# First attention: the split of the finished maxima on GpSimd instead of VectorE, and the turn of their rows four halves later

## The reference

```
B, S, D = hidden_states.shape            # 2, 1024, 128;  H = 16 heads of hd = 8
qkv = hidden_states @ w_attn + b_attn
q, k, v = split, reshaped to (B, H, S, hd)
scores = einsum('bhqd,bhkd->bhqk', q, k) * hd ** -0.5
scores = scores + mask        # -log(1 + k - q) for keys after the query, 0 at it, -inf before it
attn = softmax(scores, axis=-1)
out = (attn @ v) reshaped to (B, S, D) @ w_proj + b_proj
```

## Time and profile before

| | us |
|---|---|
| median of 3 runs | 1112.68 |
| lowest, highest | 1106.85, 1120.25 |
| the profiled execution's own time | 1102.42 |
| its span, first to last instruction | 1100.3 |
| busy in the span: PE, PEld | 896.0, 606.8 |
| busy in the span: DVE, ACT, POOL | 665.8, 427.8, 512.2 |
| mean granted TensorE clock | 0.887 of full |

### The profile page before, as it was taken

The page is one execution under the profiler, slowest core; times in us unless marked ns, Lnnn a source line. Parts: engine busy times, 40 slices in busy tenths (PEclk is TensorE's granted clock), DMA queues, the critical chain, the costliest instruction groups (busy, mean ns, idle before and its releaser), DMA issues. The chain is left out here.

```text
span 1100.3 us, 17965 instructions
## 1 busy us (share of the span) xinstructions
PE 896.0 (81%) x6334; PEld 606.8 (55%) x6334; DVE 665.8 (61%) x1876; ACT 427.8 (39%) x1024; POOL 512.2 (47%) x463
## 2 busy tenths in 40 slices
PE   4668999999999867267899699994998987389992
PEld 2122333333333356155566588994895756389982
DVE  6767778686872075879687656778003666533334
ACT  2323665565666441113111276774334211032220
POOL 5425888888898831053222344555200001156661
PEclk9657999899999988758799799997999998599997
DMA  4800110110000000001000000302000001266764
GB/s 146 257 1 1 31 31 2 30 30 19 13 2 24 1 22 8 0 15 40 1 2 1 10 21 10 134 9 77 1 1 1 1 10 30 89 188 216 217 196 145
DMA packets 38893, 55.95 MB, mean 51 GB/s; under 512 B 6954, under 2 KB 26290, under 8 KB 38678
## 3 DMA queue, kind: packets, MB, share of 16 engines
q1 hardware_dynamic: 36310, 49.70, 14.9%
q0 software_dynamic: 2496, 5.12, 1.6%
HBM read 43.66 MB, written 10.94 MB: 50 GB/s over the span
## 5 line engine op out<-in xcount | busy, mean ns | idle before, releaser
L423 POOL TENSOR_TENSOR arena<-arena 128x1024 f32<-128x1024 f32 (+3 forms) x105 | 201.0, 1946 | 42.4 <-ACT arena L598 42.3
L665 DVE CUSTOM_DVE_ANT_0 ps<-ps,arena 128x512 f32<-128x512 f32 (+3 forms) x256 | 148.7, 640 | 45.3 <-PE ps L480 44.4
L598 ACT ACTIVATE arena<-ps 128x512 f32<-128x512 f32 (+3 forms) x320 | 137.3, 491 | 89.4 <-PE ps L511 58.1
L480 PE MATMUL ps<-arena 48*128 48x512 bf16 (+3 forms) x384 | 103.9, 371 | 24.9 <-DVE arena L665 15.9
L117 POOL TENSOR_SCALAR vareps<-meanvar 128x4 f32<-128x4 f32 x32 | 7.9, 246 | 213.2 <-DVE meanvar L98 213.2
L503 PE MATMUL ps<-arena 51*128 51x512 bf16 (+3 forms) x384 | 76.0, 349 | 6.0 <-DMA arena<-arena 5.2
L2075 PE MATMUL ps<-arena 128*128 128x128 f32 x624 | 79.9, 284 | 0.0
L480 PEld LDWEIGHTS ps<-arena 48*128 48x128 bf16 x384 | 28.3, 95 | 91.3 <-DVE arena L665 55.1
L2075 PEld LDWEIGHTS ps<-arena 128*128 128x128 f32 x624 | 76.4, 200 | 0.0
L152 PE MATMUL ps<-ident,xn 128*128 128x128 f32 x128 | 26.0, 352 | 59.4 <-DVE x L921 19.9
L532 PE MATMUL ps<-arena 128*9 128x512 f32 (+3 forms) x640 | 67.7, 495 | 3.9 <-POOL arena L423 3.9
(11 more groups left out here) (341 smaller groups left out, 2081.0 us busy)
## 6 DMA issues: line engine op xcount, KB each, us to landing
arena<-in_L_ffn_w SPq DMA_DIRECT2D x39, 512.0 KB, 3.7
arena<-scratch SPq DMA_DIRECT2D x32, 192.0 KB, 4.0
arena<-in_L_ffn_w SPq DMA_DIRECT2D x16, 256.0 KB, 3.4
scratch<-arena SPq DMA_DIRECT2D x12, 256.0 KB, 4.4
arena<-expert_rows SPq DMA_DIRECT2D x8, 256.0 KB, 4.9
scratch<-arena SPq DMA_DIRECT2D x4, 384.0 KB, 5.0
scratch<-arena SPq DMA_DIRECT2D x12, 128.0 KB, 4.3
x<-in_x SPq DMA_DIRECT2D x4, 256.0 KB, 3.9
```

Of the source, the lines that this page charges most:

```text
L423: nc.gpsimd.tensor_tensor(e, e, weight[:, at:at + k].unsqueeze(1).broadcast_to([P, 2, k]), ALU.mult).then_inc(weighed, 1)
L480: nc.tensor.matmul(m.ps[:, (2 * k + e) % MAX_BANKS, 0:wd], qs[rows, u % BUFS, pair, i * P:(i + 1) * P], ks[rows, u % BUFS, pair, first:fir ...
L598: nc.scalar.activation(probs(g)[:, 2 * p + e, 0:wd], m.ps[:, BANK[h, e], 0:wd], ACT.Exp, scale=SCALE).then_inc(exps, 1)
L665: nc.vector.tensor_tensor_reduce(out=scores, in0=scores, in1=before[:, 0:wd], scale=-1.0, scalar=negrest[:, h, i:i + 1] if i < TPC else 3e ...
```

## The change

The four instructions of the split go from VectorE to GpSimd. Unit 0's split stands behind the table of logarithms and before GpSimd's first multiply. Unit u's split stands in GpSimd's own order right behind the multiply (if there is one) of the half three before its window's end (halves 11, 35, 59, 83, 107, 131, 155). `shares()` adds 1400 ns to GpSimd's account at each of these seven, so that other halves go to GpSimd: 127 of 192 instead of 133. The turn of unit u's parts stands four halves after the window's end instead of one, the copy five halves after instead of two.

```diff
@@ pieces and shares
+    SPLIT_AT = {window(u)[1] - 3: u for u in range(1, UNITS)}
+
@@ def shares():
             if pool + (1500 if diagonal(n) else 0) <= gone:
                 by_pool.add(h)
                 pool += 80 + 2.25 * k
+            if h in SPLIT_AT:
+                pool += 1400
@@ def schedule():
-        yield from ((what, 0, 0) for what in ("split", "turn_max", "take_max"))
+        yield from ((what, 0, 0) for what in ("turn_max", "take_max"))
@@
             if u:
-                for what, late in (("split", 0), ("turn_max", 1)):
-                    due.setdefault(window(u)[1] + late, []).append((what, u, 0))
-                due.setdefault(window(u)[1] + 2, []).insert(0, ("take_max", u, 0))
+                due.setdefault(window(u)[1] + 4, []).append(("turn_max", u, 0))
+                due.setdefault(window(u)[1] + 5, []).insert(0, ("take_max", u, 0))
@@ GpSimd
+    def split_maxima(pool, u):
+        pool.wait_ge(max_set, 2 * NP * (u + 1))
+        mine = negmax[:, u % 2, :, :]
+        part = lambda p: nparts[:, u % 2, :, :].rearrange("q i (h p) -> q h i p", p=3)[:, :, :, p]
+        if u >= 2:
+            pool.wait_ge(n_turned, u - 1)
+        nc.gpsimd.tensor_copy(part(0), mine).then_inc(nsplit, 1)
+        pool.wait_ge(nsplit, 3 * u + 1)
+        nc.gpsimd.tensor_tensor(nrest[:, :, :], mine, part(0), ALU.subtract).then_inc(nsplit, 1)
+        pool.wait_ge(nsplit, 3 * u + 2)
+        nc.gpsimd.tensor_copy(part(1), nrest[:, :, :]).then_inc(nsplit, 1)
+        pool.wait_ge(nsplit, 3 * u + 3)
+        nc.gpsimd.tensor_tensor(part(2), nrest[:, :, :], part(1), ALU.subtract).then_inc(nparts_set, 1)
@@ def gpsimd(pool):
-        for u in range(UNITS):
-            for n in range(NG):
-                for p in range(2):
-                    if u * HALVES + 2 * n + p in BY_POOL:
-                        weigh(pool, u, n, p)
+        split_maxima(pool, 0)
+        for h in range(UNITS * HALVES):
+            if h in BY_POOL:
+                weigh(pool, h // HALVES, h // 2 % NG, h % 2)
+            if h in SPLIT_AT:
+                split_maxima(pool, SPLIT_AT[h])
@@ VectorE
-        def split_maxima(u, _):
...
-        do = {"max": maximum, "split": split_maxima, "divide": divide}
+        do = {"max": maximum, "divide": divide}
```

## The result

The change made the kernel slower: 1117.24 us (8 runs, 1111.89 to 1129.12) against 1107.03 us (8 runs, 1098.31 to 1120.25), ratio 1.0103 [1.0072, 1.0134]. On another chip it came out at 1.0142 [1.0089, 1.0194]. The forecast was 3.0 us faster, inside 1 per cent, and its sign failed. The range of 1102 to 1118 holds 1117.24 only because the kernel before came out at 1107.03 here and at 1112.68 there: as a difference the range ended at 5.3 us slower, and 10.2 were measured (11.4 by the ratio). The profiled execution took 1121.9 us with a span of 1120.0, 19.7 more than before. Comparisons leave out runs that lie clearly above their kernel's fastest.

What follows compares the result with a forecast made beforehand. TensorE was taken to bound the middle units, GpSimd the last. Terms -0.6 + 0.2 - 1.1 - 1.0 - 0.3 - 0.2 = -3.0 us gave 1109.7 us from a median of 1112.68, range 1102 to 1118.

Steps and rivals of the forecast that it cites:

- What bounds the kernel: First attention: TensorE bounds the middle units, in order and nearly without gaps; GpSimd bounds the last unit.
- splits off VectorE: Seven windows: VectorE's 15.4 us disappear, but only 0.28 us in each of two windows comes back, -0.6 us.
- The split on GpSimd: Four small 128x32 instructions on GpSimd: 0.97 us together, about 1.2 us with three waits, bounds 0.8 and 3.2.
- First unit: The first unit's split has no cover: 1.15 us become about 1.3 on GpSimd, +0.2 us, bounds -0.2 and +2.1.
- Covered in the windows: Seven later splits: GpSimd stands idle there and the turn comes over 5 us later, so cost zero.
- Turn and copy four halves later: In six windows the copy follows without idling, 0.2 us gained in each, -1.1 us; the seventh gives -1.0.
- the bank's wait of the earlier trace: At the old place a score bank waits for ScalarE's copy behind a late turn: 3.3 us over seven windows.
- ahead of half 160: Seventh window: the last turn (0.6 us) and part of the copy (0.4) leave the path, -1.0 us.
- the last unit: From half 160 GpSimd runs without rest; one multiply fewer (0.7), last products about +0.5: -0.2 us.
- The shares: Before half 160: eleven more 256-column halves and six fewer 128-column ones by logs on TensorE, -0.3 us.
- half 13's 0.18: Price per 256-column half by logs on TensorE: half 13 lasts 2.69 us with logs, 2.51 without.
- The rival of log halves at full price: Log halves on TensorE cost +6.1 us in place of -0.3, giving 1116 us; chance 0.07.

## Why the prediction was wrong

*What bounds the kernel.* Right for the middle units. VectorE's 15 us came off without moving TensorE, and the port wait was what the forecast made of it: -0.6 forecast for splits off VectorE, -0.9 or -0.3 at like clock, by the profile of before.

*The split on GpSimd.* 1.27 us of instructions (0.33 + 0.27 + 0.33 + 0.34), 1.48 from the first's start to the last's end, against 1.2 with all waits; the casts take 0.33 where 0.22 was put on the strength of a single cast of another size and type. First unit +0.42 instead of +0.2. Covered in the windows, as forecast.

*Turn and copy four halves later: the step that failed by its instructions.* Forecast -1.1 and -1.0; beside the split alone it measured +1.4 over units 1 to 6 (split and turn late +0.5, the split alone -0.9). The copy does follow without idling, as forecast, but the bank's wait of the earlier trace rows was not there to be given back: leaving the old place gave 0.43 us in most units, less than the 0.61 us for which the transposes keep TensorE busy, and arriving took 0.64. A move that was to give 0.2 us a unit cost 0.2. Only ahead of half 160 did the move pay (-0.67 and -0.63 us in halves 15 and 17 of unit 6), and most of it was given back in halves 18, 20 and 21: -0.4 in that unit where -1.0 stood, and nothing in unit 7 (34.4 us from its first scores to the last copy, as before). GpSimd was less than full in the last unit, too, and with a pause before it:

```profile
353.73 9.06 POOL L427 TENSOR_TENSOR arena<-arena 128x1024 f32<-128x1024 f32 x6 [1.12 <-ACT arena L617]
363.28 4.73 POOL L427 TENSOR_TENSOR xnT<-xnT,arena 128x1024 f32<-128x1024 f32 x2 [0.49 <-ACT xnT L617]
```

The last copy of numerators starts at 395.43 us (380.39 before), 15.04 later, where the last unit's first scores were 15.62 later: -0.6 for the last unit against -0.2. The new shares bring it: all five profiles with them have 33.8 or 33.9 us there, all others 34.4 to 34.6.

*The shares.* Near nothing alone (-0.1 at like clock) for -0.3; beside the split more (split and shares together +0.3, the split alone -0.9), since both take away the same wait at half 15: with the new shares alone VectorE's first casts take 0.55 us at most. A 256-column half by logs cost 0.45 us in half 12, where the forecast took half 13's 0.18 for all. The rival of log halves at full price (+6.1) doesn't show half by half; what the fit says of it stands below.

*The sum.* At like clock +0.4 for the first split, +0.1 in unit 0, +1.7 or +2.1 in units 1 to 6 (the change's two profiles) and -0.6 in unit 7: about **+2 us where -3.0 stood**. That is 5 us of a miss of 14 or more. The rest is a term the sum did not have: **TensorE's granted clock**. The forecast compared two kernels at the clock of one execution and took its variation for symmetric scatter of 4 or 5 us. But the change's mean clock is 0.8751 and 0.8755, on two occasions, against 0.881 to 0.883 for before. By the Trainium skill (TensorE: Matmul & The Clock Gate, "Part 1: The HAM clock gate") the slow clock is the default that activity releases, and the monitor runs freely, not in step with the kernel. By that the trace agrees in part: whether a given unit is hit changes between executions of one program (unit 3 of before is hit in one profile of three), and in units 1 to 6 nearly all falls come behind the loosest piece of a unit; most of those in unit 7 come behind a head that is 91% busy. What the runs suggest beyond this is that being hit goes with the unit's length: extra matmuls of 0.2 and 0.4 us a unit, with the turn in its place, came with five hit units and a clock of 0.875 and 0.873 (+-0.004 and 0.003). The change lengthened a unit at full clock from 36.4 or 36.7 to 37.1 us. It is not shown: the split alone with the first on VectorE has before's lengths and a clock of 0.8771, the change with its first split on VectorE has the change's lengths and 0.8816.

The account closes roughly by the profiles. A low stretch of 10.2 us costs a unit 3.9 us and one of 3.4 us 1.45. The two profiles of the change thus hold 10.7 and 9.2 us of it in units 1 to 6, the three of before 5.3, 0 and 0, in the mean 1.8: some 8 us, which with the 2 us of instructions makes 10, where 1.0103 and 1.0142 are 11.4 and 15.6. Counted directly, the last copy of numerators begins 14.0 us later in the mean of the change's two profiles than in that of before's three: 0.4 ahead of unit 0, 3.7 in unit 0 (most of it the long low stretch of one profile), 10.5 in units 1 to 6, -0.6 in unit 7. Behind it the two kernels take the same (723.8 and 722.9 us in the mean), but from 719.9 to 727.6 in before's three alone.

By the runs it closes less well. At equal mean clock the fit leaves 6.2 us of the change, and it sorts the kernels by a term that the like-clock sums put near nothing: those with the new shares lie 3.4 (shares alone), 4.2 (with the split), 4.6 and 6.2 us above before, those with the old shares and no added matmuls between -1.5 and +2.3. So the shares may have cost some 3 us more than the half-by-half comparison shows; no run here says where.

Three things stay open: that cost, why a unit of 37.1 us should meet the low clock more often than one of 36.5, and why the change with its first split on VectorE was faster than this account allows.

## What to carry to other kernels

Relieving an engine pays where another waits for it at that moment: of a blocked instruction of 2.5 us 0.3 came back, and of 15 us of busy time no more than 0.9. A move within TensorE's own order should be priced by starts, half against half, at both places. And where a loop of tens of us has one loose piece per turn, profile both kernels several times and compare granted clocks before judging instructions: here 3 us of extra matmuls came with 12 us. And a delay put in on purpose has to be measured in its own trace before anything is concluded from it: eight and twenty memsets made 0.11 and 0.24 us.

## What the runs showed of the hardware

A low stretch of 10.2 us costs a unit 3.9 us (unit 3 of before: 40.33 with it, 36.45 without), one of 3.4 us about 1.4 (unit 1 of the change: 38.44 and 37.03). In unit 6 of the change TensorE fell to half clock after 4.8 us in which it had been busy 75% of the time and some 2 us at 87%, and stayed there through 10 us in which it was busy almost without a gap. Unit 3 of before, with the same head, did so in one execution and ran at full clock throughout in two others. VectorE's cast of 128x32 takes 0.24 us alone and took up to 2.54 us beside GpSimd's multiplies. GpSimd's cast of 128x32 to bf16 takes 0.33 us, longer than its sum of that size (0.27) and than VectorE's cast (0.24).
